# Head attention: queries and keys as two float32r parts, score products in pairs of row halves

## The reference, cut to what matters

```
xn = layernorm(x)
q, k, v = heads(xn @ Wq.T) / 4, heads(xn @ Wk.T), heads(xn @ Wv.T)   # 16 heads of 16
scores = q @ k.T + rel[:, clip(i - j, 0, 128)], masked where i < j
attn = softmax(scores)
out = x + (attn @ v) @ Wo.T
```

## Time and profile before

| | us |
|---|---|
| median of 3 runs | 2771.97 (2771.16 to 2774.59) |
| the profiled execution | 2777.85 |
| its span | 2776.0 |
| PE busy in the span | 2217.6 (80%) |
| DVE busy | 1620.4 (58%) |
| ACT busy | 969.2 (35%) |
| Pool busy | 453.9 (16%) |

### The profile page before, as it was taken

The page is one execution under the profiler, slowest core; times in us unless marked ns, Lnnn a source line. Parts: engine busy times, 40 slices in busy tenths (PEclk is TensorE's granted clock), DMA queues, the critical chain, the costliest instruction groups (busy, mean ns, idle before and its releaser), DMA issues.

```text
span 2776.0 us, 39998 instructions
## 1 busy us (share of the span) xinstructions
PE 2217.6 (80%) x13342; PEld 1613.4 (58%) x13342; DVE 1620.4 (58%) x4577; ACT 969.2 (35%) x1964; POOL 453.9 (16%) x402
## 2 busy tenths in 40 slices
PE   4489999908999857999994276378999999999476
PEld 2478888806888736888883144324444454444254
DVE  6744443353555675433444897266866766875695
ACT  4122233203333331232331331325555556556321
POOL 4320000040000134000003553411011011000242
PEclk8799999958999878999997555669999999999755
DMA  7110101020000122001002100242322323230001
GB/s 237 41 59 26 28 28 32 22 76 1 1 1 1 35 83 73 28 28 32 28 28 60 49 12 0 61 65 59 48 42 53 48 47 63 37 43 2 5 22 39
DMA packets 83735, 114.14 MB, mean 41 GB/s; under 512 B 12162, under 2 KB 74020, under 8 KB 80420
## 3 DMA queue, kind: packets, MB, share of 16 engines
q1 hardware_dynamic: 77396, 94.53, 15.5%
q0 software_dynamic: 6144, 17.05, 1.9%
HBM read 68.90 MB, written 42.64 MB: 40 GB/s over the span
## 4 chain that ended last, share of the span: by engine, by line
PE 63%; DVE 21%; ACT 5%; issue 5%; DMA 3%; POOL 2%; another core or an unknown queue 1%; SPq 0%; ACTq 0%; DVEq 0%; POOLq 0%
PE psum L774 9%; PE psum L776 9%; PE psum L775 9%; PE psum L122 5%; PE psum L2097 4%; PE psum L123 4%; PE psum L124 4%; PE psum L2076 4%; PE psum L2056 3%; PE psum L861 3%; PE psum L2080 3%; DVE junk L1961 2%; PE psum L1426 2%; DVE m L1949 1%; DVE stats L155 1%
## 5 line engine op out<-in xcount | busy, mean ns | idle before, releaser
L1898 ACT ACTIVATE pt<-psum 128x512 f32<-128x512 f32 (+3 forms) x768 | 338.9, 491 | 283.2 <-DVE psum L1987 196.2
L739 DVE SCALAR_TENSOR_TENSOR h<-psum,xg,sg 128x128 f32<-128x128 f32 x592 | 166.9, 345 | 415.2 <-PE psum L861 415.2
L774 PE MATMUL psum<-w_hi,xt_hi 128*128 (+1 forms) x720 | 286.3, 398 | 33.7 <-DVE xt_lo L704 33.7
L548 ACT ACTIVATE sg<-psum 128x512 f32<-128x512 f32 x180 | 107.6, 598 | 584.0 <-PE psum L776 543.0
L775 PE MATMUL psum<-w_lo,xt_hi 128*128 (+1 forms) x720 | 284.5, 395 | 0.0
L776 PE MATMUL psum<-w_hi,xt_lo 128*128 (+1 forms) x720 | 284.5, 395 | 0.0
L2056 PE MATMUL psum<-ks,qs 96*128 96x512 bf16 (+3 forms) x768 | 232.9, 342 | 49.7 <-DMA ks<-qk_scr 19.9
L2076 PE MATMUL psum<-qs,ks 99*128 99x512 bf16 (+3 forms) x768 | 236.8, 332 | 18.4 <-ACT pt L1898 11.4
L774 PE MATMUL psum<-w_hi,ht_hi 128*128 (+1 forms) x720 | 220.5, 306 | 8.3 <-DVE x L754 8.0
L1961 DVE CUSTOM_DVE_ANT_0 junk<-psum,band_q 128x256 bf16<-128x256 f32 (+1 forms) x512 | 204.8, 400 | 22.3 <-PE psum L2056 12.0
L776 PE MATMUL psum<-w_hi,ht_lo 128*128 (+1 forms) x720 | 205.9, 286 | 0.0
(11 more groups left out here) (281 smaller groups left out, 4884.4 us busy)
## 6 DMA issues: line engine op xcount, KB each, us to landing
xg<-w_dram SPq DMA_DIRECT2D x54, 256.0 KB, 3.3
qk_scr<-parts SPq DMA_DIRECT2D x32, 384.0 KB, 2.5
qs<-qk_scr SPq DMA_DIRECT2D x96, 128.0 KB, 7.0
ks<-qk_scr SPq DMA_DIRECT2D x96, 128.0 KB, 7.7
xg<-rows_in SPq DMA_DIRECT2D x74, 132.0 KB, 2.2
rows_out<-yb SPq DMA_DIRECT2D x74, 128.0 KB, 1.7
x<-x_dram SPq DMA_DIRECT2D x4, 1024.0 KB, 9.3
out_dram<-x SPq DMA_DIRECT2D x4, 1024.0 KB, 4.4
```

Of the source, the lines that this page charges most:

```text
L739: ins = dve.scalar_tensor_tensor(out=h[i % 2][:, e, :], in0=u[:, e, :], scalar=xg[j % XSLOT][:, at:at + 1], in1=sg[i % 2][:, e, :], op0=AL ...
L774: pe.matmul(out, a[0], b[0], start=first, stop=False)
L1898: act.activation(pt[n % NPT][:, 0:q1 - q0], st_bank(n)[:, 0:q1 - q0], ACT.Exp).then_inc(*exped.up())
```

## The change

Queries and keys are kept as two float32r parts, high and rest. Three combinations of parts (high high, high rest, rest high) make 48 rows a head, and two more hold the row maximum: 50 rows. Heads 0 and 1 of a group lie in partitions 0 to 49, heads 2 and 3 in 64 to 113, and products of two heads in different halves of the rows stand side by side in the order. ACT's second cast and Pool's subtraction of `qk` are gone, as are a `max_rest` and a `max_part`.

The step of `attend` is now two scores, then groups of maxima (pairs too), then the bands of both (`band`). `lead` is 1.4 and a step takes as many groups as bring the stream up to it; projections advance every second step of 24. `load` and the second half of `max_out` are issued by Pool instead of SP, the latter as two DMAs. The ones are written by a Pool copy into partitions 32 to 63 and 96 to 127 of each `ks`, for buffers 1 and 2 after load 0 and load 1. The DVE operation of L1961 writes to the bank it reads, and waits no more for the one before it.

```diff
-        HEAD_OF = (HG - 1, *range(HG - 1))
+        HALF_ROWS = P // 2
+        PAIR = HG // 2
+        HEAD_OF = (HG - 1, 1, 2, 0)
+        QK_PARTS = [(0, 0), (0, 1), (1, 0)]
+        ROWS = DH * len(QK_PARTS)
+        NPART = 2
...
             def maxima(u):
-                first = [("max_zero", u)]
-                for h in range(HG):
+                yield [("max_zero", u)]
+                for hh in range(PAIR):
                     for i in QORDER:
-                        step = [("max_far", (u, h, i))] if spans(i)[3] else []
-                        yield first + step + [("max", (u, h, i))]
-                        first = []
+                        if spans(i)[3]:
+                            yield [("max_far", (u, half * PAIR + hh, i)) for half in range(2)]
+                        yield [("max", (u, half * PAIR + hh, i)) for half in range(2)]
...
-                    for pos in range(HG):
-                        yield [("score", (u, cell, pos))]
+                    for pos in range(0, HG, 2):
+                        yield [("score", (u, cell, pos)), ("score", (u, cell, pos + 1)), ("band", (u, cell, pos))]
...
-            order = sum(project(0), []) + [("load", u) for u in range(min(NR, NHG))]
+            order = [("ones", 0)] + sum(project(0), []) + [("load", 0)]
+            for u in range(1, NR):
+                order += [("ones", u), ("load", u)]
...
-            more()
-            order.append(("ones", 0))
-            steps, lead = HG * NCELL, 1.5
-            per_u = HG * BT + 7
+            steps, lead = PAIR * NCELL, 1.4
+            per_u = ends[0] + 1
...
-                    order.extend(tokens)
                     if tokens[0][0] == "value":
+                        order.extend(tokens)
                         placed.add(tokens[0])
                         continue
-                    if taken[0] < (u + lead + step / steps) * per_u:
+                    order.extend(tokens[:2])
+                    while taken[0] < min((u + lead + step / steps) * per_u, len(stream)):
                         more()
+                    order.extend(tokens[2:])
                     order.extend(next(tail, []))
-                    if step % 3 == 0:
+                    if step % 2 == 0:
                         order.extend(next(proj, []))
...
+                        elif kind == "load":
+                            b, g = divmod(i, NHG)
+                            slot = i % NR
+                            pool.wait_ge(*ones_ok(2 * slot + 2))
...
+                            if i >= NR:
+                                pool.wait_ge(*score((i - NR + 1) * NCELL * HG))
+                            for s0, pair in enumerate(QK_PARTS):
+                                for n, dst in enumerate((qs[slot], ks[slot])):
+                                    for half in range(2):
+                                        r0 = half * HALF_ROWS + s0 * DH
...
+                                        pool.dma_start(dst[r0:r0 + DH, :, :].rearrange("p h s -> p (h s)"),
...
                         elif kind == "ones":
-                            pool.wait_ge(*max_zero(1))
-                            for r, k in enumerate(ks):
-                                pool.memset(k[KS_ROWS:KS_ROWS + MROWS, :, :], 1.0).then_inc(*ones_ok.up())
-                                pool.wait_ge(*ones_ok(r + 1))
...
+                            for half in range(2):
+                                rows = slice(half * HALF_ROWS + MQ, half * HALF_ROWS + 2 * MQ)
+                                pool.tensor_copy(ks[i][rows, :, :], unit[rows, :].unsqueeze(2).to_broadcast(
+                                    [MQ, PAIR, SEQ])).then_inc(*ones_ok.up())
+                                pool.wait_ge(*ones_ok(2 * i + half + 1))
...
-                            act.activation(parts[:, 1, o, :], rests[o][:, :], ACT.Copy).then_inc(*part1.up())
...
-                            if n:
-                                dve.wait_ge(*near_max(n))
+                            banded = bank[:, far - cut:w - cut]
                             dve.tensor_tensor_reduce(
-                                junk[:, 0:bw], bank[:, far - cut:w - cut],
-                                band_q[:, u % NHG * HG + h, 2 * P - bw:2 * P], 1.0, LOWEST, ALU.add, ALU.max,
-                                m3[u % 2][:, h * BT + t, 2:3]).then_inc(*near_max.up())
+                                banded, banded, band_q[:, u % NHG * HG + h, 2 * P - bw:2 * P], 1.0, LOWEST, ALU.add,
+                                ALU.max, m3[u % 2][:, h * BT + t, 2:3]).then_inc(*near_max.up())
...
-                            pe.matmul(bank[:, 0:c1 - c0], qs[r][0:KS_ROWS, h, t * P:(t + 1) * P],
-                                      ks[r][0:KS_ROWS, h, c0:c1], start=True,
+                            r0, hh = half_of(h)
+                            pe.matmul(bank[:, 0:c1 - c0], qs[r][r0:r0 + ROWS, hh, t * P:(t + 1) * P],
+                                      ks[r][r0:r0 + ROWS, hh, c0:c1], start=True,
...
+                        elif kind == "band" and near_of[i[1]]:
+                            u, cell, pos = i
+                            for m in range(pos, pos + 2):
+                                n, j, c, h, q0, q1, b1 = cell_of((u, cell, m))
+                                if h < HP:
+                                    for part in range(3):
+                                        ins = pe.matmul(st_bank(n)[:, 0:b1 - q0], identb[:, :],
+                                                        band[:, part, u % NHG, h, q0 - j * P:b1 - j * P],
+                                                        start=False, stop=(part == 2))
+                                    ins.then_inc(*score.up())
```

More of the change, by code:

```diff
@@ L1718, in attention_heads @@
             PROJ, NPT = 3 * KD, 3 * HG
-            normed, added, scaled, turned, xt_hi, xt_full, xt_lo, proj = (S(x) for x in (
-                "normed", "x_added", "xn_scaled", "turned", "xt_hi", "xt_full", "xt_lo", "proj"))
-            part0, rest_ok, part1, part2, v1_ok = (S(x) for x in ("part0", "rest", "part1", "part2", "v1"))
-            rest_used = S("rest_used")
+            normed, added, scaled, turned, xt_full, xt_lo, proj = (S(x) for x in (
+                "normed", "x_added", "xn_scaled", "turned", "xt_full", "xt_lo", "proj"))
+            qk_hi, qk_lo, v1_ok = (S(x) for x in ("qk_hi", "qk_lo", "v1"))
             max_zero, far_ok, far_max, near_ok, near_max, row_max = (S(x) for x in (
@@ L1840, in on_pool @@
                         elif kind == "ones":
-                            pool.wait_ge(*max_zero(1))
-                            for r, k in enumerate(ks):
-                                pool.memset(k[KS_ROWS:KS_ROWS + MROWS, :, :], 1.0).then_inc(*ones_ok.up())
-                                pool.wait_ge(*ones_ok(r + 1))
+                            if i == 0:
+                                pool.memset(unit[:, :], 1.0).then_inc(*S("unit").up())
+                                pool.wait_ge(*S("unit")(1))
+                            else:
+                                pool.wait_ge(*xt_lo(KD * CB))
+                            for half in range(2):
+                                rows = slice(half * HALF_ROWS + MQ, half * HALF_ROWS + 2 * MQ)
+                                pool.tensor_copy(ks[i][rows, :, :], unit[rows, :].unsqueeze(2).to_broadcast(
+                                    [MQ, PAIR, SEQ])).then_inc(*ones_ok.up())
+                                pool.wait_ge(*ones_ok(2 * i + half + 1))
                 def on_act():
@@ L2075, in on_pe @@
-                            by_pe = near_of[cell] and h < HP
-                            ins = pe.matmul(bank[:, 0:q1 - q0], ks[r][:, h, j * P:(j + 1) * P], qs[r][:, h, q0:q1],
-                                            start=True, stop=not by_pe)
-                            if by_pe:
-                                for part in range(3):
-                                    ins = pe.matmul(bank[:, 0:b1 - q0], identb[:, :],
-                                                    band[:, part, u % NHG, h, q0 - j * P:b1 - j * P],
-                                                    start=False, stop=(part == 2))
@@ L2083, in on_pe @@
-                            ins.then_inc(*score.up())
+                            r0, hh = half_of(h)
+                            ins = pe.matmul(st_bank(n)[:, 0:q1 - q0], ks[r][r0:r0 + ROWS + NPART, hh, j * P:(j + 1) * P],
+                                            qs[r][r0:r0 + ROWS + NPART, hh, q0:q1], start=True,
+                                            stop=not (near_of[cell] and h < HP))
+                            if not (near_of[cell] and h < HP):
+                                ins.then_inc(*score.up())
[8 more added lines that the diff above has]
+                                                        start=False, stop=(part == 2))
+                                    ins.then_inc(*score.up())
```

98 lines of the change are left out of this document (41 added, 57 removed).

## The result

The changed kernel takes 2981.0 us (median of 4 runs, 2966.7 to 2998.4), the kernel before 2773.3 beside it: a ratio of 1.075, 95% interval 1.068 to 1.082. The forecast was 2800, the range 2740 to 2850: the time is 208 us above the kernel before and 131 above the range's upper end. The profiled execution took 2969.97 us, span 2968.2.

The account below looks back on a forecast made before the run. PE was taken to bound a quiet unit, DVE next. Terms: -31 quiet units, -9 projection's chain, +24 start, +7 catch-up, +37 later projection halves, +28 us on 2771.97, so 2800 us; range 2740 to 2850.

Parts of the forecast that it names:

- The pairs: TensorE's maxima and scores: a pair costs one product, -7.1 us a unit, of which 54 tiling changes give back 2.9.
- The waits: TensorE in a quiet unit: second products start late, +1 us, and scores wait for exponentials on three banks, +1.1.
- The quiet unit: A unit without projection: -2.1 us, to 35.7; over the 14.6 units with maxima -31 us.
- R4: Rival: Pool's loads cost 1.25 us and ACT's pauses drop TensorE's clock: +57, 2829 us; shares the forecast's 0.55.
- the projection's chain: Projections: ACT's second cast and Pool's second subtraction before each DMA go, so PE waits less: -9 us.
- R3: Rival: paired products take turns and don't run together, +65 for -31, 2896 us; chance 0.08.
- Pool's price: Loads moved from SP to Pool: 0.95 us to issue each, bounds 0.46 and 1.25.
- (a): Start of the heads stage: Pool's queue of loads and fills delays DVE's first maximum to 1835.9: +24 us.
- (b): First pair of scores: catching up 22 pieces of maxima puts 12 us of DVE before the first band; net +7.
- (c): Five later projection halves: Pool's add stands behind twelve loads, ACT waits before its scale: +37 us.
- R1: Rival: Pool issues as fast as SP (0.46 us): -18, 2754 us, faster; chance 0.27.
- What would show it: Signs in the profile; an issue under 0.6 us, or a quiet unit at 34 or 42, makes the prediction wrong.

Follow-up runs that it names:

- e1: Streams of products only, rest of the kernel left out, single products, halves and pairs of several shapes: 300 paired products in 34.3 us, 0.114 each against 0.226.
- e5: Eight streams of products, A to H, made like the kernel's steps, with nothing else of the kernel: 1.34 us a step in A, 3.19 in B.
- G: Stream of e5: four float32r pairs of 512 columns, then a wait for ScalarE; kept the clock with PE busy 81% of its window.
- A: Stream of e5: a step like the changed kernel's, pairs of 48 float32r rows and bands, values every second step, no waits: 1.34 us a step.
- C: Stream of e5: A with products over 96 bfloat16 rows in place of float32r pairs, no waits: 1.38 us a step.
- e10: e4's kernel with all 64 rows of a half in every score and maxima product: 2903.57 us, +130.2 against the kernel before.
- e2: Kernel before with the changed order alone (score pairs, maxima pairs, then bands, lead 1.4), bfloat16 96 rows, SP's loads: 2853 us, +74.5.
- e9: Kernel before with maxima in pairs, new order of heads, lead 1.4 and catch-up, bands ahead of maxima, scores single: 2802.44 us, +29.1.
- e12: Changed kernel with all 64 rows of each half and zero products ahead of each head's bands: +147.9 us against the kernel before.
- e4: Changed kernel's float32r halves and Pool loads with the order of before (layout alone): 2988.69 us, +210.0 against the kernel before.
- e6: Changed kernel with all 64 rows of each half in every product for scores and maxima: 2929.46 us, +156.2 against the kernel before.
- B: Stream of e5: A with one short wait for ScalarE ahead of the second pair, 48 rows: 3.19 us a step.
- F: Stream of e5: B with 64 rows and not 48 in each product: 2.07 us a step.
- e16: Kernel before with the lead of 1.4 and the catch-up alone, products single, in the old order: -0.3 us against the kernel before.
- e14: e3's kernel timed in 3 rounds beside e13: 2979.8 us, ratio 1.0728 to the kernel before.
- e13: The changed kernel timed again, unaltered, beside e14: 2981.1 us, ratio 1.0754 to the kernel before.
- e3: Changed kernel with the unit's loads and the maxima's return issued by SP through float32 views: 2963.2 us, +184.5 against the kernel before.

## Why the forecast was wrong, step by step

**The pairs** (a pair of 512 columns at one product's price, -7.1 us a unit; changes of tiling 0.1 each way, +2.9). The mechanism was right: two halves side by side (e1), 0.10 for the change out of half rows, and 51 changes of tiling in a unit without a projection (2478.40 to 2536.60) where I had counted 54. Missing was the start of the second pair behind such a change: 0.33 us and not 0.23 (2149.15 to 2149.48), so a group of score pair and maxima pair pays some 0.1 a third time. It is paid once a group and not once a pair, as e1's steps of two pairs and e5's stream G of four show:
```profile
610.62 0.73 PE L62 MATMUL ps<-r 48*128 48x512 f32 x4
611.28 0.83 PE L64 MATMUL ps<-b 128*128 128x256 bf16 x6
```
```profile
840.91 1.20 PE L47 MATMUL ps<-r 48*128 48x512 f32 x8 [0.32 <-ACT e L69]
842.03 0.23 PE L67 MATMUL ps<-b 128*32 128x128 bf16 x1
```
Two pairs take 0.66 us to the next start and four 1.12: 0.23 each and 0.2 on top both times. I had taken the values' column strips for this, and within one x8 group no such start occurs. A against C gives -1.0 us a unit where I had -4.2; 24 such starts are some 2.4 of the 3.2 between them.

What single halves pay at the full clock is seen in PE's order of time in e10, to set against the earlier trace rows:
```profile
2421.83 0.33 PE L2084 MATMUL psum<-qs,ks 64*128 64x384 f32 x1
2422.10 0.50 PE L2095 MATMUL psum<-band,identb 128*128 128x256 bf16 x3
2422.53 0.33 PE L2065 MATMUL psum<-ks,qs 64*128 64x128 f32 x1
```
0.27 for 384 columns (0.16 at 2.4 GHz) going out, 0.43 for three bands (0.32) coming in. Such a unit has 79 changes of tiling, counted in the trace, where the kernel before has 24: 55 more at 0.11 are 6.0 of the 6.3 us of 44.1 against 37.8.

**The waits** (+1 for the second product, +1.1 for the new wait). The mechanism, two requests at a time on three banks, fits the waits of e2, and the size was wrong: +5.8 us a unit. I had priced one wait in nine cells by the exponential's chain; the pairs of maxima, to which I gave no term of their own, are 2.4 of it (e9).

**The quiet unit**, -2.1 in the sum. At the full clock e12's two, less the 2.4 of zeros, are 43.8 and 44.8: +6 to +7. The two terms above give -1.0 + 5.8 = 4.8; the other 1 to 2 are not accounted for. Over 14.6 units that is 88 to 102 us.

**The clock.** The step that failed most is one that the sum doesn't have. Every price was taken at 2.4 GHz, as the earlier trace rows show it, and R4 let the clock fall only in pauses of ACT that Pool would make. The 208 us less 88 to 102 and less 5 at the start leave 101 to 115 us that come with the lower clock, or 7.5 more, since the projection's chain gained as much. That is a remainder, not a measurement; e10 against e4 (80 us), e6 against the changed kernel (52, with the clock still at 0.84) and the 98 us estimated from e12 show such sizes more directly. What the runs show in place of the forecast's fixed price is a clock that falls under waits together with few rows (e5, B against A and F). The condition of R3's price (+65 for -31) didn't come, and yet the loss was larger than its 2896.

**Pool's price** (0.95 a load, bounds 0.46 to 1.25). It was 0.49: the lower bound, SP's row, and not Pool's own indirect DMA. (a) The fill was 3.84 against 4.7 forecast, and the first maximum came +2.0 in the trace, +5.3 from the stage's start, instead of +24. (b) The catch-up at the first scores: ACT waited 11.4 us for the first band against 12 forecast. e16 shows that in the order of before the catch-up costs nothing in the end. (c) The additions do stand right behind the loads (1922.46, 1923.44), with 5.8 us of issuing and not 11.4 ahead of them, and ACT never stands idle before its scale (24 of them, 0.0 us), where I had named five pauses of 5 to 10 us; e14 against e13 leaves 1.4 us for what moving loads and maxima's return costs, where (a) and (c) had 61. R1's condition was met in full, and its 2754 failed by the quiet unit and the clock.

The Trainium skill (DMA: Bandwidth & Descriptors) was cited for why the loads must leave SP. e3 and e14 issue them from SP through float32 views, without a change of time, so that reason doesn't bind here.

**The projection's chain** (-9). PE's wait for DVE's part was 11.0 us in five; in the same view of after it is 3.5, also in five:
```profile
PE psum L2065 <- DVE parts L1950: 3.5, 5, 0.9
```
Right, with 7.5 of the 9.

**What would show it** named two ways to be wrong, an issue under 0.6 us and a quiet unit at 42. Both came, the unit at 43.8 and 44.8 by e12. With the unit's full-clock time in the sum (+95 for -31), 5 at the start, 7.5 gained in the chain and nothing for (b) and (c), the forecast would have been near 2865, still some 116 short. That the time rose, as the forecast had at 0.60, is no success of it: its cause, Pool's issues, isn't there. The chance of faster was also added up wrongly: 0.27 and a third of 0.10 are 0.30, not 0.32.

## What to carry to other kernels

Before packing products into halves of the array, ask how many rows will be at work in the same time once they are packed, not only how long PE is busy: here a stage that held 2.4 GHz lost it when its TensorE work was made thinner and its waits more. Price each excursion into half rows at three parts (in, the second pair's later start, out; some 0.1 us each here), and set it against what a pair saves: with one or two short pairs at a time almost nothing is left. With three banks for each kind, as here, single issues in turn were faster than issues in twos (37.8 us a unit against 43.6).

## What the runs showed of the hardware that I had not expected

- Rows that compute nothing hold the clock: 14 to 16 more of them in each product for scores and maxima, clock 0.81 to 0.93 and 80 us less in the same program (e4, e10); in a stream with the same waits 0.50 for 48 rows and 1.00 for 64 (e5, B and F).
- Products in one half only lose the clock without any gap between them (0.54), and pairs of 128 columns too (0.55), while pairs of 512 hold it (e1). Single halves between products over all rows kept it as well (e5, E).
- Behind a change of tiling the second pair of float32r products starts 0.33 us after the first for 512 columns, the third and later ones 0.23 (e5, G).
- A direct DMA of 128 KB in 16 rows costs Pool 0.49 us to issue, about what it costs SP (0.42) and half of an indirect one (0.95).
